# Local attention: block-diagonal q, one score product per head pair, and weights loaded once per layer

## The reference

```
for i in range(DEPTH):                       # DEPTH = 6
    x = attn_layer(shift_tokens(x), Wqkv[i], q_scale[i], k_scale[i], Wo[i]) + x
    x = ffn_layer(shift_tokens(x), ln_g[i], ln_b[i], W1[i], b1[i], W2[i], b2[i]) + x

def attn_layer(x, Wqkv, qs, ksc, Wo):        # 16 heads of 64, windows of 32 tokens
    q, k, v = split(x @ Wqkv)
    q, k = l2norm(q) * qs, l2norm(k) * ksc
    q, k = rotary(q) * scale, rotary(k) / scale
    # window w of q against windows w-1 and w of k
    sim = einsum('bhwie,bhwje->bhwij', bq, bk2) * QK_SCALE
    sim = where(mask, -max, sim)
    attn = softmax(sim, -1)
    return einsum('bhwij,bhwje->bhwie', attn, bv2) @ Wo
```

## Time and profile before

| | |
|---|---|
| median of 3 runs | 4658.14 us (4657.95 to 4670.21) |
| the profiled execution | 4670.98 us, its span 4669.2 us |
| mean granted TensorE clock | 0.959 of full speed |
| PE busy | 4135.5 us (89%), 67078 instructions |
| PE weight loads | 2766.5 us (59%), 67078 instructions |
| DVE busy | 2915.5 us (62%) |
| POOL busy | 2805.6 us (60%) |
| ACT busy | 2616.0 us (56%) |
| DMA | 258.77 MB, mean 55 GB/s |

### The profile page before, as it was taken

One profiled execution on the slowest core, in us unless ns is written; L12 is line 12 of the kernel. 1 busy time (PEld: TensorE's weight loads), 2 busy tenths in 40 slices (PEclk: granted clock), 3 DMA queues, 4 the chain that ended last, 5 costly groups with the idle time before them and its releaser, 6 DMA issues. The chain is left out here.

```text
span 4669.2 us, 162098 instructions
## 1 busy us (share of the span) xinstructions
PE 4135.5 (89%) x67078; PEld 2766.5 (59%) x67078; DVE 2915.5 (62%) x4217; ACT 2616.0 (56%) x4417; POOL 2805.6 (60%) x3584
## 2 busy tenths in 40 slices
PE   5879788689999999999999999999999999999994
PEld 2434344346666666666666666666666666666663
DVE  5565656466666666666666666666666666666664
ACT  2545353446666656656656566566665656656552
POOL 0000000177777777777777777777777777777771
PEclk8989798889999999999999999999999999999997
DMA  0000000112222222222222223222222222222223
GB/s 28 3 15 2 15 2 15 41 39 65 65 70 74 58 68 67 72 55 67 66 70 64 56 68 79 62 59 70 68 72 55 65 66 70 64 56 67 70 64 81
DMA packets 284568, 258.77 MB, mean 55 GB/s; under 512 B 122871, under 2 KB 258508, under 8 KB 271148
## 3 DMA queue, kind: packets, MB, share of 16 engines
q1 hardware_dynamic: 283820, 248.14, 20.0%
HBM read 117.63 MB, written 29.77 MB: 32 GB/s over the span
## 5 line engine op out<-in xcount | busy, mean ns | idle before, releaser
L787 DVE TENSOR_TENSOR products<-bank_d,table 128x1024 f32<-128x1024 f32 x772 | 938.1, 1216 | 684.4 <-ACT sq L614 679.7
L910 POOL TENSOR_TENSOR products<-products 128x2048 f32<-128x2048 f32 x192 | 871.0, 4536 | 313.8 <-DVE products L787 313.8
L413 PE MATMUL bank_d<-w_qkv,xT 128*128 128x512 f32 x1544 | 807.5, 626 | 18.7 <-issue 13.0
L614 ACT ACTIVATE sq<-bank_d 128x512 f32<-128x512 f32 x772 | 468.0, 606 | 469.9 <-PE bank_d L413 457.4
L947 POOL TENSOR_TENSOR qk_rot<-products,rnorm 128x2048 f32<-128x2048 f32 x192 | 695.6, 3623 | 14.0 <-POOL rnorm L929 12.7
L785 DVE TENSOR_REDUCE ss<-sq 128x16 f32<-128x1024 f32 x386 | 468.8, 1214 | 229.3 <-ACT sq L614 229.3
L874 POOL MEMSET ident<- 128x128 f32 x1 | 0.2, 205 | 915.1 <-POOLq L1064 915.1
L954 POOL TENSOR_TENSOR prob<-prob,inv_sum 128x1024 f32<-128x1024 f32 x192 | 365.4, 1903 | 307.3 <-DVE inv_sum L767 307.3
L1491 DVE TENSOR_REDUCE part_max<-s_max 128x1 f32<-128x512 f32 (+3 forms) x768 | 399.5, 554 | 152.2 <-PE s_max L1240 101.3
L478 PE MATMUL scores<-kT,qT 64*32 64x64 f32 x24576 | 430.4, 218 | 24.4 <-issue 24.4
L413 PE MATMUL bank_a<-w_qkv,xT 128*128 128x512 f32 x768 | 403.1, 607 | 49.7 <-ACT gate L669 47.5
(11 more groups left out here) (168 smaller groups left out, 7581.9 us busy)
## 6 DMA issues: line engine op xcount, KB each, us to landing
v_back<-v SPq DMA_DIRECT2D x96, 768.0 KB, 5.4
w_qkv<-in_Wqkv_dram SPq DMA_DIRECT2D x25, 1024.0 KB, 5.1
v_back<-v SPq DMA_DIRECT2D x192, 128.0 KB, 5.7
w_qkv<-in_Wqkv_dram SPq DMA_DIRECT2D x25, 512.0 KB, 5.4
xs<-x_layers SPq DMA_DIRECT2D x194, 64.0 KB, 2.1
w_o<-in_Wo_dram SPq DMA_DIRECT2D x24, 512.0 KB, 6.9
xr<-x_layers SPq DMA_DIRECT2D x96, 128.0 KB, 3.0
x<-x SPq DMA_DIRECT2D x96, 128.0 KB, 1.8
```

Of the source, the lines that this page charges most:

```text
L413: nc.tensor.matmul(bank[:, :], xT[:, P * a:P * (a + 1)], w_qkv[:, col:col + 512], start=True, stop=True).then_inc(d_filled if i < 8 else a ...
L614: nc.scalar.activation(sq[j % 2][:, 8 * c:8 * c + 8, :], bank_d[slot][:, :].rearrange("p (h d) -> p h d", d=DH), ACT.Square).then_inc(squa ...
L787: nc.vector.tensor_tensor(products[:, a, head:head + 8, :, :].rearrange("p h r (o d) -> p h r o d", o=2), bank[:, :].rearrange("p (h r d) ...
L910: link(nc.gpsimd.tensor_tensor(products[:, a, :, 0, :], products[:, a, :, 0, :], products[:, a, :, 1, :], ALU.add))
```

## The change

Two independent edits.

**Weights once per layer.** `Step` now knows its layer, its sequence b and its position p. The loads of a round are done only in the first or the last sequence of a layer, and so are the waits for them. The rotary table is made only in the last sequence of a layer, for the next layer. On POOL the two L899 instructions stand in 4 of the 16 steps of a layer, before in all 16.

**Scores.** `qT` becomes block diagonal: for each head pair and window there are 64 columns, 32 for each head, and the rows of the other head are zero. They are zeroed once at the start by DVE. One product then takes all 128 rows (both heads) and 64 columns (both heads' queries), with the same 64 keys. A block has 16 such products in place of 32. The rows of the score bank are sorted by tile a and then by head (before: by head and then by tile), which the products with v and the mask follow. ACT has to copy each q bank in two halves, 64 rows each, because the two heads go to different columns.

```diff
@@ rounds, Step: Step(layer, b, p) in place of Step(f, p)
-        qT = sb("qT", [P, HP, PAIR])
+        qT = sb("qT", [P, HP, PAIR // WINDOW, 2, WINDOW])
...
-                if runs(now) and s.p == 0:
-                    sp.wait_ge(table_ready, POS * (s.f + 1))
-                    load_qk_rows(s.f + 1)
-                if runs(now) and s.p == POS - 1:
+                if runs(now) and s.b == 0 and s.p == 0:
+                    sp.wait_ge(table_ready, POS * (s.layer + 1))
+                    load_qk_rows((s.layer + 1) % DEPTH)
+                if runs(now) and s.b == BATCH - 1 and s.p == POS - 1:
                     sp.wait_ge(d_filled, chunk_at(now, 7)[1] + 1)
-                    load_w_qkv(s.f + 1, 0, 2 * INNER, wqk_in)
+                    load_w_qkv((s.layer + 1) % DEPTH, 0, 2 * INNER, wqk_in)
...
-                        for h2 in range(2):
-                            for a in range(2):
-                                win = 4 * a + 2 * u + ph
-                                row = 32 * (2 * h2 + a)
-                                last = nc.tensor.matmul(
-                                    scores[row:row + 32, hp, u, :],
-                                    qT[64 * h2:64 * h2 + 64, hp, 32 * win:32 * win + 32],
-                                    kT[pair.par][64 * h2:64 * h2 + 64, hp, 32 * win:32 * win + 64],
-                                    start=False, stop=True, skip_group_check=True)
+                        for a in range(2):
+                            win = 4 * a + 2 * u + ph
+                            last = nc.tensor.matmul(
+                                scores[64 * a:64 * a + 64, hp, u, :],
+                                qT[:, hp, win, :, :].rearrange("p h q -> p (h q)"),
+                                kT[pair.par][:, hp, 32 * win:32 * win + 64],
+                                start=False, stop=True, skip_group_check=True)
...
                 if kind == 0:
-                    out = qT[:, hps, P * a:P * (a + 1)]
+                    for h2 in range(2):
+                        rows = slice(DH * h2, DH * (h2 + 1))
+                        out = qT[rows, hps, 4 * a:4 * a + 4, h2, :]
+                        ins = nc.scalar.activation(out, bank[rows, :, :].rearrange("p j (w q) -> p j w q", q=WINDOW), ACT.Copy)
+                    ins.then_inc(a_free, 1)
...
-                nc.scalar.activation(out, bank, ACT.Copy).then_inc(a_free, 1)
+                    nc.scalar.activation(out, bank, ACT.Copy).then_inc(a_free, 1)
...
             nc.vector.memset(v[1][:, :, :], 0.0)
+            nc.vector.memset(qT[:, :, :, :, :], 0.0)
...
-                    make_table(s.f + 1, s.p)
+                    if s.b == BATCH - 1:
+                        make_table(s.layer + 1, s.p)
```

More of the change, by code:

```diff
@@ L119, in __init__ @@
         self.f = step.f + q // POS
+        self.layer = step.layer + (step.b + q // POS) // BATCH
         self.n = step.t - lag
@@ L350, in step @@
                                      .rearrange("(a t) d -> t a d", a=2)).then_inc(xs1_in[back2.par], 16)
-                if runs(back2) and s.p == 1 and in_rounds(s):
-                    load_wo(s.f)
+                if runs(back2) and s.b == 0 and s.p == 1 and in_rounds(s):
+                    load_wo(s.layer)
                 if runs(now):
@@ L370, in step @@
                                  .rearrange("(a t) d -> t a d", a=2), x2[back3.par][:, :, :]).then_inc(x2_out, 16)
-                    if s.p == 2 and in_rounds(s):
-                        load_ffn(s.f)
+                    if s.b == 0 and s.p == 2 and in_rounds(s):
+                        load_ffn(s.layer)
             rounds(sp, step)
@@ L486, in times_wo @@
             def times_wo(s):
-                if s.p == 2:
-                    pe.wait_ge(wo_in, 16 * (s.f + 1))
+                if s.b == 0 and s.p == 2 and in_rounds(s):
+                    pe.wait_ge(wo_in, 16 * (s.layer + 1))
                 pe.wait_ge(a_free, ring_a.at(prev(s), "O11")[1] + 1)
@@ L559, in step @@
                 if runs(back3):
-                    if s.p == 3:
-                        pe.wait_ge(wffn_in, 64 * (s.f + 1))
+                    if s.b == 0 and s.p == 3:
+                        pe.wait_ge(wffn_in, 64 * (s.layer + 1))
                     ffn_up(s, "gA")
@@ L686, in step @@
                 if runs(back3):
-                    if s.p == 3:
-                        act.wait_ge(wffn_in, 64 * (s.f + 1))
+                    if s.b == 0 and s.p == 3:
+                        act.wait_ge(wffn_in, 64 * (s.layer + 1))
                     bank = filled(s, "xn")
@@ L725, in _ @@
             act.wait_ge(constants_ready, INIT)
-            copy_x(Step(-1, POS - 1))
+            copy_x(Step(-1, BATCH - 1, POS - 1))
             for i in range(EARLY):
-                square(Step(-1, POS - 1).pair(-1), i)
+                square(Step(-1, BATCH - 1, POS - 1).pair(-1), i)
             rounds(act, step)
@@ L775, in rotate @@
                 if i == 0:
-                    dve.wait_ge(table_ready, pair.n + 1)
+                    dve.wait_ge(table_ready, POS * pair.layer + pair.p + 1)
                 slot, n = chunk_at(pair, i)
@@ L829, in step @@
                 if runs(back3):
-                    if s.p == 3:
-                        dve.wait_ge(wffn_in, 64 * (s.f + 1))
+                    if s.b == 0 and s.p == 3:
+                        dve.wait_ge(wffn_in, 64 * (s.layer + 1))
                     hidden_units(s, "A")
```

63 lines of the change are left out of this document (32 added, 31 removed).

## The result

| | before | after |
|---|---|---|
| median of 4 runs | 4658.49 us (4657.95 to 4670.21) | 4952.59 us (4945.86 to 4958.39) |
| profiled execution, its span | 4670.98 us, 4669.2 us | 4945.86 us, 4944.0 us |
| undisturbed step | 36.72 us | 39.47 us |
| mean granted TensorE clock | 0.959 | 0.961 |

The ratio is 1.062 (95%: 1.0601 to 1.0639): 6.2% slower, 294 us by the medians and 275 us between the two profiled spans. The forecast was 4800 us, in a range from 4750 to 4900 us. The sign was right, the size was not.

The account below looks back on a forecast made before the run. PE, in order and waiting for ACT, was taken as the bound. The profiled 4671.0 us + 159 (copies) + 0 - 20 (fetches) gave 4810, against the median 4797, rounded to 4800 us; range 4750 to 4900 us.

Parts of the forecast that it names:

- What bounds the kernel: Whole step: PE is the fullest engine, 34.82 of 36.73 us, and otherwise waits for ACT's `kT` and `yT`.
- Copies of q: ACT ahead of the first score block: eight half copies at 0.48 us delay `kT` by 1.66 us a step, +159 us.
- Height costs nothing, elements in a row count: ACT's q copies: a half with 64 rows but 512 elements in each was taken at a whole copy's 0.48 us.
- The rival of half the time: ACT's q copies: time goes by rows, so eight halves cost what four copies do; 4638 us, 4% chance.
- PE's waits: PE ahead of the first score block: wait for `kT` from 0.29 to about 1.2 us, small new waits at transposes.
- Score products: PE's score blocks: a block stays at 1.03 us with half the instructions; 0 us, bounds -10 to +15.
- The two rivals on blocks: PE's score blocks: 0.52 us by instruction count (4700 us), or about 1.9 us run serially (4970 to 5140 us); 4% each.
- Fewer instructions to fetch: PE's instruction queue: 18% fewer products and loads cut 108 us of lost time by 20 us, bounds 0 and -60.
- Weights once per layer: DMA loads and POOL's table: already hidden, so making them less often gives 0 us.
- The zeroed tile: DVE at the start: clearing the new `qT` once costs under 5 us even if nothing hides it.
- own range: Whole kernel: 4755 to 4845 us, from -0.3 to +0.2 us a step on the copies and the fetch bounds.
- The clock: PE ahead of the scores: idle gaps lower the granted clock to 0.59; 4940 us, or 4870 in half the steps; 15% chance.

Follow-up runs that it names:

- half_copies: Kernel before with only each q bank copied in two halves of 64 rows, same `qT` and products; 4920.46 us against 4665.17.
- gapped_whole: Kernel before with whole q copies written into the changed `qT` layout, 32 columns used and 32 free; 4658.85 us against 4661.82.
- half_grouped: Kernel before with q copied in halves, two banks together: both upper halves, then both lower; 4959.67 us against 4665.17.
- merged_no_split: Kernel before with the merged products and whole q copies into the first head's columns, second head's left zero; 4721.34 us against 4661.82.
- weights_only: Kernel before with only the weight and rotary-table loads made once per layer, scores unchanged; 4692.77 us against 4665.17.
- reordered: Kernel before with ACT's order changed: small last-window `kT` copies behind the third square, `yT` ahead of the second exponentials; 4686.77 us against 4661.82.

## Why the prediction was wrong, point by point

- **What bounds the kernel** was read rightly. PE works its queue off in order, and the first score block waits for ACT's last copy of `kT`; half_copies, which changes ACT alone, makes the step 2.65 us longer.
- **Copies of q: the step that failed.** The term was 4 x 0.48 - 0.26 = 1.66 us a step, 159 us. The mechanism is as written, and the stand-still of 0.26 us went as written. The size of a half copy was wrong. It was bounded from above by the distance between whole copies, 0.48 us, but that is a distance between neighbours that overlap; their own length, about 0.6 us, would have been the better upper bound. With 0.61 us for each of eight it is 8 x 0.61 - 4 x 0.48 - 0.26 = 2.70 us; measured 2.66, in half_copies too, 255 us over 96 steps. That is 96 us of the miss. The upper end of the range failed with it: "-0.3 us a step to +0.2 on the copies" should have reached to +1.0.
- **Height costs nothing, elements in a row count**: right (592 ns at 64 rows, 598 at 128). The rival of half the time is out. Neither the gaps (gapped_whole) nor the height but the change of the start row costs time (half_grouped, and L1376 and L1384 of the kernel before).
- **PE's waits.** 1.16 us ahead of the first block, as forecast at 1.2. The new waits at the transposes, 0.42 and 0.90 us, were forecast as small. The forecast of the first came out by luck, since the further delay is in the second kind.
- **Score products.** Taken at 0, bounds -10 to +15 us; measured +0.06 us a block, +0.10 us a step, 10 us. The two rivals on blocks (0.52 us, or 1.9 us) are out.
- **Fewer instructions to fetch.** The fetches fell by 17% as forecast, the lost time did not: 113 us in the profile against 109, where the sum had -20 us. The step from "fewer fetches" to "less lost time" failed. It took all 108 us for such waits, where they are 80 us and part of the rest is the clock; they fell to 66 us, but merged_no_split, with as few fetches, has 87, so that fall is no proof of the rule. That is 24 us of the miss.
- **Weights once per layer.** 0 in the quiet step, as forecast; POOL's 100 us less busy time as well. In the median weights_only is 28 us slower, which no term of the sum had. It is not in the quiet steps; that the changed code moved the fetches would fit, but is not shown.
- **The zeroed tile.** Forecast at under 5 us; 3.47 us on DVE, but beside it one of POOL's eight selects on the mask took 4.86 us instead of 0.71, PE's first transpose waits for them, and the start is 5 us later.
- **The sum** was 4797 us before rounding, 156 below the result: 96 from the copies, 24 from the fetches, 10 from the blocks, 10 from the start and the end, 19 from where the two profiled executions lie to their medians, less 3 for 95 steps instead of 96. The range, up to 4900, rested on the copies' upper bound and on the clock, and neither reached this far. The prediction's "own range" of 4755 to 4845 does not come out of the terms that it names either: with 29 and 40 us below and 19 and 20 us above, it would be 4728 to 4836.
- **The clock** stayed at 1.00 in quiet steps, with gaps of up to 1.16 us in each; that rival had 15%. It falls in some long steps, in the kernel before as in the changed one (44 and 41 us of missing clock).

## What to carry to other kernels

Bound a new instruction from above by its own length in the timeline, not by the distance at which overlapping neighbours follow each other, and ask whether the new order keeps what lets them overlap. Splitting a copy by rows saved no time on ACT here and cost more than twice as much (1.22 us against 0.48); if it must be done, put copies with the same start row together. Packing two products into one brought nothing here, where each part of the array was left with as many instructions as before. Compare all steps of a loop and not its quietest: reordered won 0.57 us there and lost more in the others. And time an edit of a long looped program in more than one placement, since 128 instructions ahead of everything cost 0.8%.

## What was new about the hardware

- Two ACTIVATEs in a row overlap by 0.12 us if they start at the same row, and not at all if one starts at row 0 and the next at row 64 or the other way round: 0.48 to 0.50 us from start to start against 0.59 to 0.62 us, at 512 fp32 elements in a row from PSUM. The number of rows does not matter: 96 rows and then 128 from the same start overlap.
- A zeroing of 4096 elements a row on DVE (3.47 us) held one select on POOL for 4.86 us; the eight take 10.85 us together, in the kernel before 6.71 us, and so in every run with and without the zeroing.
- PE's waits for no other engine cost 80 us in 56 waits in the kernel before. Cutting the DMA traffic of every step's `v_back` copies to a sixteenth brought them to 36 us in 42 waits; the fetches stayed 550.
- Behind a wait of 3.15 us the granted clock was 0.50 for 6.8 us, so that the wait cost about as much again.
